# Attention with dense queries: 32-row score matmuls, the maximum pass masked on VectorE, the batch loop written out

## The reference, cut to what matters

```
def _L1_attn_ref(x, w_in, b_in, w_out, b_out):
    B, S, E, H = (2, 256, 128, 16)
    hsz = esz // H
    qkv = x @ w_in.T + b_in
    q, k, v = jnp.split(qkv, 3, axis=-1)
    q, k, v = (to_heads(q), to_heads(k), to_heads(v))
    scale = np.float32(1.0 / np.sqrt(hsz))
    scores = jnp.einsum('bhqd,bhkd->bhqk', q * scale, k)
    causal_bias = jnp.where(jnp.tril(jnp.ones((slen, slen), dtype=bool)), 0.0, -jnp.inf).astype(x.dtype)
    scores = scores + causal_bias
    attn = jax.nn.softmax(scores, axis=-1)
    out = jnp.einsum('bhqk,bhkd->bhqd', attn, v)
    out = out.transpose(0, 2, 1, 3).reshape(bsz, slen, esz)
    out = out @ w_out.T + b_out
```

## Time and profile before

| | |
|---|---|
| median of 3 runs | 2952.7 us (2952.65 to 2961.28) |
| profiled execution: span from first to last instruction | 3037.0 us |
| the same execution's time beside the span | not listed apart; the span is 84.3 us above the median |
| mean granted TensorE clock | 0.932 |
| TensorE matmuls busy | 2549.4 us, 84% of the span |
| VectorE busy | 2285.1 us, 75% |
| ScalarE busy | 1790.3 us, 59% |
| GpSimd busy | 1373.7 us, 45% |

### The profile page before, as it was taken

The page is one execution under the profiler, slowest core; times in us unless marked ns, Lnnn a source line. Parts: engine busy times, 40 slices in busy tenths (PEclk is TensorE's granted clock), DMA queues, the critical chain, the costliest instruction groups (busy, mean ns, idle before and its releaser), DMA issues. The chain is left out here.

```text
span 3037.0 us, 38397 instructions
## 1 busy us (share of the span) xinstructions
PE 2549.4 (84%) x11128; PEld 1669.2 (55%) x11128; DVE 2285.1 (75%) x3877; ACT 1790.3 (59%) x3099; POOL 1373.7 (45%) x1486
## 2 busy tenths in 40 slices
PE   6888477888888888868887689969988889887999
PEld 5766233343344344227676568746555556554887
DVE  6887478989999999998786544478777777774444
ACT  3566465657556656524666445547777667665555
POOL 2365488888988988961563630021121121111000
PEclk9999688999999999998998789979999999998999
DMA  2246222222222222221345200020000000001000
GB/s 69 55 130 123 79 68 67 75 69 72 70 74 74 77 73 74 77 71 39 75 130 96 73 21 1 0 95 1 1 1 1 2 1 1 1 1 39 7 8 14
DMA packets 99804, 152.38 MB, mean 50 GB/s; under 512 B 12940, under 2 KB 50572, under 8 KB 99028
## 3 DMA queue, kind: packets, MB, share of 16 engines
q1 hardware_dynamic: 82052, 98.41, 10.6%
q0 software_dynamic: 17040, 51.07, 6.8%
q10 hardware_dynamic: 512, 0.53, 0.1%
HBM read 131.08 MB, written 18.87 MB: 49 GB/s over the span
## 5 line engine op out<-in xcount | busy, mean ns | idle before, releaser
L1750 POOL TENSOR_TENSOR a_hc<-a_H,a_cb 128x512 f32<-128x512 f32 x512 | 620.0, 1233 | 134.3 <-DVE a_H L1614 127.3
L1406 PE MATMUL a_Y<-a_hc,ident 128*128 128x512 f32 x1024 | 535.3, 633 | 57.0 <-POOL a_hc L1750 48.6
L2216 DVE TENSOR_REDUCE a_mx<-a_W 128x1 f32<-128x512 f32 (+3 forms) x768 | 397.2, 550 | 153.3 <-PE a_W L2005 99.6
L2116 ACT ACTIVATE a_pt<-a_W 128x512 f32<-128x512 f32 (+3 forms) x768 | 353.5, 493 | 224.1 <-PE a_W L2018 220.7
L1532 ACT ACTIVATE a_dA<-a_dt,a_aneg 128x512 f32<-128x512 f32 x512 | 342.6, 714 | 193.8 <-POOL a_dt L1769 103.2
L1406 PEld LDWEIGHTS a_Y<-a_hc,ident 128*128 128x128 f32 x1024 | 183.0, 196 | 307.6 <-POOL a_hc L1750 212.7
L1638 DVE TENSOR_TENSOR a_BX<-a_u,a_BX 128x1024 f32<-128x1024 f32 x256 | 308.6, 1211 | 44.0 <-PE a_BX L1340 22.3
L1614 DVE TENSOR_TENSOR_SCAN a_H<-a_dA,a_H,a_BX 128x512 f32<-128x512 f32 x256 | 312.5, 1264 | 2.5 <-ACT a_dA L1532 2.5
L2018 PE MATMUL a_W<-a_Q,a_K 128*128 128x512 f32 (+3 forms) x768 | 302.3, 399 | 4.1 <-ACT a_pt L2116 2.0
L1614 DVE TENSOR_TENSOR_SCAN a_H<-a_dA,a_BX 128x512 f32<-128x512 f32 x256 | 296.7, 1202 | 1.1 <-POOL a_hc L1750 1.0
L2002 PE MATMUL a_W<-a_K,a_Q 128*128 128x512 f32 (+3 forms) x768 | 273.9, 363 | 20.4 <-DVE a_K L2283 9.9
(11 more groups left out here) (327 smaller groups left out, 5628.4 us busy)
## 6 DMA issues: line engine op xcount, KB each, us to landing
a_cb<-a_crow SPq DMA_DIRECT2D x256, 256.0 KB, 3.1
m_orows<-m_yt SPq DMA_DIRECT2D x46, 256.0 KB
a_Q<-attention_zeros POOLq DMA_DIRECT2D x3, 2048.0 KB, 13.3
t_wst<-ternary_w SPq DMA_DIRECT2D x22, 256.0 KB, 2.7
m_xrows<-m_pool SPq DMA_DIRECT2D x16, 256.0 KB, 2.3
m_xg<-m_xrows,m_gidx POOLq DMA_INDIRECT x184
out<-x SPq DMA_DIRECT2D x8, 256.0 KB, 2.3
m_wg<-moe_ws SPq DMA_DIRECT2D x2, 516.0 KB, 4.5
```

The lines of the kernel that those rows point to most:

```text
L1406: pe.matmul(Y[:, h, :], ident[:], hc[:, g % HCRING, :], start=False, stop=v == NS - 1).then_inc(s_y, 1)
L1750: pool.tensor_tensor(hc[:, G % HCRING, :], H[:, s, span], cb[:, v % RING, :], ALU.mult).then_inc(s_hc, 1)
L2116: act.activation(pt[:, u % PR, 0:BLK - r * P], W[:, 3 + u % 3, 0:BLK - r * P], ACT.Exp).then_inc(s_exp, 1)
L2216: dve.tensor_reduce(dst, W[:, s % 3, 0:min(BLK, (t + 1) * P - c * BLK)], AX, ALU.max)\
```

## The change

In the attention:

- Q becomes as dense as K: one tile for each group, its four heads stacked. Both score matmuls contract over the 32 partitions of their head, in Q and in K.
- With that go the copies head by head (`queries`), the stacked tile `stk`, the zeros by DMA and the memset of Q. `stack` writes Q directly. The maximum is added to Q by one instruction of 128 partitions.
- The mask matmul (L2005) goes, with its operands. Where a piece of the maximum pass lies on the diagonal, VectorE adds the mask and takes the maximum with `tensor_tensor_reduce`, which writes the masked scores to a new tile `masked` and the maximum to `mx`. The mask is 512 columns wide now, 384 zeros ahead of the triangle. Pieces off the diagonal keep `tensor_reduce`.
- K is projected ahead of Q, in the prologue and in each group.
- The loop over batches 1 and 2 is written out.

```diff
@@ slot_uses
-            uses.update({-7: ("xT", 0, 0, 0), -6: ("xT", 0, 0, 1), -5: ("Q", 0, 0, 0), -4: ("Q", 0, 0, 1),
-                         -3: ("K", 0, 0, 0), -2: ("K", 0, 0, 1), -1: ("V", 0, 0, 0)})
+            uses.update({-7: ("xT", 0, 0, 0), -6: ("xT", 0, 0, 1), -5: ("K", 0, 0, 0), -4: ("K", 0, 0, 1),
+                         -3: ("Q", 0, 0, 0), -2: ("Q", 0, 0, 1), -1: ("V", 0, 0, 0)})
...
-            uses.update({0: ("Q", rel, n, 0), 2: ("Q", rel, n, 1), 4: ("K", rel, n, 0), 5: ("K", rel, n, 1),
+            uses.update({0: ("K", rel, n, 0), 2: ("K", rel, n, 1), 4: ("Q", rel, n, 0), 5: ("Q", rel, n, 1),
...
@@ all_slots
-        with eng.Fori(1, NBATCH - 1) as i:
+        for i in range(1, NBATCH - 1):
...
-        Q, K = sb("Q", [P, GROUPS * GH, SEQ], F32R), sb("K", [P, GROUPS, SEQ], F32R)
+        Q, K = sb("Q", [P, GROUPS, SEQ], F32R), sb("K", [P, GROUPS, SEQ], F32R)
...
@@ TensorE, max_unit
-                    out = W[:, s % 3, 0:cols]
-                    mm = pe.matmul(out, Q[:, g * GH + j, tile(t)], K[:, g, c * BLK:c * BLK + cols],
-                                   start=True, stop=not diag)
-                    if diag:
-                        mm = pe.matmul(W[:, s % 3, cols - P:cols], idr[:], mneg[:], start=False, stop=True)
-                    mm.then_inc(s_S, 1)
+                    pe.matmul(W[:, s % 3, 0:cols], Q[head(j), g, tile(t)], K[head(j), g, c * BLK:c * BLK + cols],
+                              start=True, stop=True).then_inc(s_S, 1)
@@ TensorE, exp_unit
-                    pe.matmul(W[:, 3 + u % 3, 0:BLK - r * P], K[:, g, tile(kt)],
-                              Q[:, g * GH + j, c * BLK + r * P:(c + 1) * BLK],
+                    pe.matmul(W[:, 3 + u % 3, 0:BLK - r * P], K[head(j), g, tile(kt)],
+                              Q[head(j), g, c * BLK + r * P:(c + 1) * BLK],
@@ ScalarE
-                    last = act.activation(Q[head(j), n * GH + j, chunk(c)], stk[head(j), c, :], ACT.Copy)
...
@@ VectorE, max_unit
-                    dve.tensor_reduce(dst, W[:, s % 3, 0:min(BLK, (t + 1) * P - c * BLK)], AX, ALU.max)\
-                       .then_inc(s_max, 1)
+                    cols = min(BLK, (t + 1) * P - c * BLK)
+                    if last:
+                        dve.tensor_tensor_reduce(masked[:, s % 3, 0:cols], W[:, s % 3, 0:cols], mask[:, BLK - cols:],
+                                                 1.0, LEAST, ALU.add, ALU.max, dst).then_inc(s_max, 1)
+                    else:
+                        dve.tensor_reduce(dst, W[:, s % 3, 0:cols], AX, ALU.max).then_inc(s_max, 1)
@@ VectorE, m_read
-                    if kind == "max" and j < 2:
-                        for jj in (2 * j, 2 * j + 1):
-                            q = Q[head(jj), n * GH + jj, chunk(c)]
-                            ins = dve.tensor_tensor(q, q.bitcast(F32), M[head(jj), :], ALU.add)
-                        if j == 1:
-                            last = ins
+                    if kind == "max" and j == 0:
+                        q = Q[:, n, chunk(c)]
+                        last = dve.tensor_tensor(q, q.bitcast(F32), M[:], ALU.add)
@@ GpSimd
-                for dst, src in ZEROS:
-                    pool.dma_start(dst, src).then_inc(s_zero, 16)
...
-                pool.memset(Q[:, 0:GH, :].bitcast(F32), 0.0).then_inc(s_cst, 1)
```

More of the change, by code:

```diff
@@ L1795, in attention @@
     ROWS = P // GH
+    LEAST = -3.0e38
     NCH, TPS = SEQ // BLK, SEQ // P
@@ L1846, in attention @@
             for st, gs in SLOTS.items()}
[L1847 to L1851, removed]
     WEIGHT = {"M": lambda k: 1, "D": lambda k: k not in ("Q", "K", "oT"), "A": lambda k: k in ("Q", "K", "oT"),
@@ L1895, in has_max, with all_slots @@
         return stage != "tail" and not (stage == "last" and g + 1 == GROUPS)
-    def all_slots(slot, eng):
+    def all_slots(slot):
         slot("pre", 0, -1)
@@ L1920, in attention @@
         wo, bo = sb("wo", [P, P]), sb("bo", [P, P])
-        mask = sb("mask", [P, P])
-        idr, mneg = sb("idr", [P, P], F32R), sb("mneg", [P, P], F32R)
-        stk = sb("stk", [P, 2, BLK])
+        mask, masked = sb("mask", [P, BLK]), sb("masked", [P, 3, BLK])
         mhalf, zero = sb("mhalf", [P, TILES]), sb("zero", [P, TPB, GH])
@@ L1948, in attention @@
         s_ld, s_cst, s_wh, s_pre = sem("ld"), sem("cst"), sem("wh"), sem("pre")
-        s_zero, s_bsc = sem("zeros"), sem("bsc")
+        s_bsc = sem("bsc")
         s_mv, s_ve, s_rstd = sem("mv"), sem("ve"), sem("rstd")
@@ L1962, in attention @@
                  (mask[:], w["mask"]))
-        ZEROS = tuple((Q[:, n:n + GH, :].rearrange("p h c -> p (h c)"), w["zeros"].bitcast(F32R))
-                      for n in range(GH, GROUPS * GH, GH))
         def early(v):
@@ L2040, in m_use @@
                     if early(v):
-                        if kind == "Q" and c == 0:
+                        if kind == "K" and c == 0:
                             pe.wait_ge(s_Md, through("D", stage, i, g, v - 1))
@@ L2097, in slot @@
                             m_use(stage, i, g, v, uses[v])
-                all_slots(slot, pe)
+                all_slots(slot)
             @block.scalar
@@ L2145, in m_read @@
                             act.activation(oT[:, c, :], M[:], ACT.Copy).then_inc(s_Ma, 1)
[L2147 to L2154, removed]
-                    last = act.activation(Q[head(j), n * GH + j, chunk(c)], stk[head(j), c, :], ACT.Copy)
-                    if j == GH - 1:
-                        last.then_inc(s_q, 1)
                 def slot(stage, i, g):
@@ L2173, in slot @@
                                 m_read(stage, i, before[1], before[2], before[0], j)
-                            copied = copies(stage, g, v)
-                            if copied:
-                                queries(i, copied, j)
-                all_slots(slot, act)
+                all_slots(slot)
             @block.vector
@@ L2275, in stack @@
                     G = (i + rel) * GROUPS + n
-                    m, k = (c, n) if kind == "Q" else (2 + c, GROUPS + n)
+                    m, k = (c, GROUPS + n) if kind == "K" else (2 + c, n)
                     dve.wait_ge(s_Ma, through("A", stage, i, g, v))
-                    if kind == "Q":
-                        wait(dve, s_q, 2 * (G - 1) + c + 1)
-                        out = stk[:, c, :]
-                    else:
-                        out = K[:, n, chunk(c)]
+                    out = (K if kind == "K" else Q)[:, n, chunk(c)]
                     dve.scalar_tensor_tensor(out, qh[:, m % 2, :].bitcast(F32), low[:, k:k + 1],
@@ L2313, in _ @@
                 chain = [None]
-                all_slots(slot, dve)
+                all_slots(slot)
             @block.gpsimd
@@ L2373, in slot @@
                             mask_step(i, g, v)
-                all_slots(slot, pool)
+                all_slots(slot)
         ph.clear()
@@ L2525, in attention_layout @@
         "w_out": g("w_out").T, "b_out": np.broadcast_to(g("b_out"), (P, P)),
-        "mask": np.triu(np.full((P, P), -1e30, np.float32), 1), "zeros": np.zeros((P, 4096), np.float32),
+        "mask": np.pad(np.triu(np.full((P, P), -1e30, np.float32), 1), ((0, 0), (3 * P, 0))),
     }
```

15 lines of the change are left out of this document (5 added, 10 removed).

## The result

The changed kernel takes 3078.3 us (median of four runs, 3070.2 to 3084.4) against 2955.3 for the kernel before beside it: a ratio of 1.0414 (95% interval 1.0392 to 1.0436), 123 us slower. The forecast was 187 us slower. The direction and the cause (TensorE's clock falls) are as forecast, the size is two thirds of it.

A forecast was written before the change was run, and what follows sets the result against it. TensorE was taken to bound the attention at 45.1 us a group. At low clock for nine tenths, 57.3 us: 16 x 12.2 - 5 - 3 = 187 us slower, 3140 us median, range 2850 to 3250 for 8 in 10 runs.

The forecast's parts named there:

- The clock decides: Attention: TensorE's clock falls to 0.50 for nine tenths of it, as score matmuls leave three quarters of the rows idle.
- The price of a group at the low clock: Attention: one group of four heads takes 59.2 us at clock 0.50, or 67 without overlap.
- three slots for four: Score matmuls: only neighbours of different heads overlap, so four take three slots; 31.0 us a group becomes 23.2.
- the overlap was undervalued: Sign for the score matmuls: holds if the clock falls and TensorE's group is under 52 us.
- shape changes 5.4: TensorE, a group at low clock: array-shape changes cost 12 x 0.28 + 2.0 us, the latter for some 10 new pairs.
- the wait for GpSimd 2.6: Attention: TensorE's wait for GpSimd's causal mask before the value matmuls stays, 41.3 / 16 = 2.6 us a group.
- the forecast's 40 us: Attention at clock 1.00: VectorE bounds at 36 us, with a tenth of loss 40 us a group.
- the 8 us of gains: Once per run: 5 us less from ScalarE's Q copies in the prologue, 3 us from the written-out batch loop.
- the rival of the scan's rate: VectorE becomes the bound: add-and-maximum at the scan's rate, 46.5 us of work a group, 3023 us; chance 0.12.
- TensorE sets the pace: Attention before the change: TensorE bounds each 45.1 us group; VectorE and ScalarE have about 10 us of slack.
- Low clock in two thirds of the attention: Fast end of the low-clock forecast's own range: 3060 us.
- in a quarter of it: Rival that gain and loss cancel, with low clock in about a quarter of the attention: 2945 to 2961 us; chance 0.08.

The follow-up runs named there:

- the mix from 72 rows up: Kernel before, score matmuls of heads 0 and 1 contracted over 72 rows, head 2 over 96, head 3 over 128: 3005.1 us, ratio 1.0187.
- equal filling with 128 and with 32 rows: Changed kernel plus two overwritten 512-column matmuls ahead of each step's first exp matmul, 24 a group: 3035.5 us with 128 rows, 3231.2 us with 32.
- the filling carried into the wait: Changed kernel plus 30 overwritten full-height matmuls a group, four issued while TensorE waits for ScalarE ahead of V's projection: 2953.1 us, ratio 0.9996.
- that experiment: Kernel before with VectorE's mask and the batch loop written out, plus nine overwritten full-height matmuls a group where its clock fell: 2954.8 us, ratio 0.9996.

## Why the prediction was right, and which term was mis-sized

**The clock decides: right.** It was to be below 0.7 and was 0.57; it was to be low for nine tenths of the attention and was for 86%. That idle rows do it was an argument then and is shown now in three ways: by the rows in the kernel before (32 and 64 rows, which bring changes of shape too, and the mix from 72 rows up, which brings nothing else), by equal filling with 128 and with 32 rows, and by the loss that vanishes with the clock restored. The reason given for it, that the change also takes work away, falls: the clock is as low with no mask matmul removed and with no overlap.

**The price of a group at the low clock: mis-sized, and this is where the 64 us lie.** The sum was 59.2 us. Its terms by the trace after:

- score matmuls 23.2 by "three slots for four": the trace shows two for one, 31.0 / 2 = 15.5. The prediction named this as its weak point ("the overlap was undervalued"), though for a group under 52 us; at 52.7 its sign stayed silent, because the next term hid the error.
- shape changes 5.4: the pair around a value step and the 10 new pairs were sized at the full clock, 0.28 us and less. At the low clock a pair takes 0.94 / 2 = 0.47, and 22 of them 10.3.
- the wait for GpSimd 2.6: 13.5 us in all, 0.8 a group, since a slower TensorE arrives later.
- value 15.5 and projections, V and transposes 12.5 stand.

Together 54.6 instead of 59.2. With the forecast's 40 us for the 14% at full clock this gives 0.86 x 54.6 + 0.14 x 40 = 52.6, where 52.7 was measured. That it agrees so closely is in part luck: the price of a change of shape comes from one step, no run shows the 40 us, and the group at the low clock in the section on the result takes 55.6 us (the longest, from 2170.9 to 2230.7 us, 59.8). Two errors partly cancelled: 7.7 us too much for scores, 4.9 too little for shapes; 1.8 more came from the wait. Over 16 groups the forecast of 57.3 was 74 us too high, and the 8 us of gains that hardly came (below) were set against it.

**VectorE: right, and cheaper than taken.** Add-and-maximum 687 ns for the 0.68 us forecast, the short part 82 ns for 0.15 us. Its work of 30.6 us a group never came near the bound, and the rival of the scan's rate (46.5 us) is refuted. The forecast of 36 also started from an early group's 35.3 where the mean of before is 534.5 / 16 = 33.4.

**ScalarE, prologue and loop: nothing where 8 us were forecast.** From the first transpose to the first exponential the prologue took 52.5 us instead of 54.0, a gain of 1.5 for the 5 forecast. TensorE's clock in it was 0.53 for 0.68 before, so what the copies alone were worth isn't shown. The loop alone gave nothing that can be told from noise.

**"TensorE sets the pace": too strong.** 40 us a group was the price if the clock held. The mask matmuls' 3.5 us a group were 1.6 us of TensorE's busy time in the kernel with only VectorE's mask, and it gained 0.4 at most. In the changed kernel with the filling carried into the wait, groups without a fall take 42.6 to 44.7 us, and the mean is 44.3. Whether the change would reach 40 us at a high clock without any filling stays untested, since no kernel here kept the clock without it.

**Two side sums are off.** Low clock in two thirds of the attention gives 3068 us by the prediction's own terms, not 3060, and in a quarter of it 2940, just outside the 2945 to 2961 given. Neither touches the forecast.

**What stays open.** How rows are weighed: 64 rows gave 0.50 throughout and the mix of 72, 96 and 128 gave 0.92, and no run separates the row count from the shape changes that 64 rows also bring. And what exactly replaces TensorE as the limit once it is relieved: the waits for GpSimd's mask and VectorE's Q grew by 13 us together, and they account for only half of the 24.7 us that it was relieved of. Whether short falls of the clock are free is open too, as said at that experiment.

## What to carry to other kernels

Before narrowing a contraction to save zeros or copies, count what share of the array's rows TensorE keeps at work: a matmul over 32 or 64 rows takes as long as one over 128 (at the low clock 512 columns over 32 rows 0.42 us to the next start, 256 over 64 rows 0.22, 512 over 128 rows 0.42), and a stretch made of them can drop to 1.2 GHz although the engine is at matmuls 95% of the time. Read the granted clock beside the busy share, and if they disagree, test with matmuls whose result is overwritten, once full height and once narrow. In these runs row slices next to each other paid only where different heads followed in pairs and no full-height matmul came between them.

## What was not expected of the hardware

- Exp and maximum matmul of one head share rows and stand next to each other in the program (e m e m), and yet the trace shows both exps at once, then both maxima. The Trainium skill (TensorE: Matmul & The Clock Gate, Part 3) gives a speedup of 3.07 for four row tiles; here pairs pass two for one.
- What counts for the clock is how many rows the instruction covers, not how many hold something: in the kernel before 96 of a score matmul's 128 rows of Q are zero, and its clock is 0.98.
- 64 rows are no better for the clock than 32, and slower in all (1.2093 against 1.1815).
- More work on the busiest engine made the kernel faster: 30 full-height matmuls a group took 125 us off the changed kernel.
- A full-height mask matmul between narrow ones cost far more than its columns: 1.02 us where the three matmuls' columns are worth 0.43.
- The read of the accumulator behind an add-and-maximum takes 82 ns, about half of the 154 ns of the 128x1 copy in the earlier trace rows.
- A higher clock need not be faster: from 0.96 to 0.99, with nine more matmuls a group, the time moved by less than 0.2%.
